# A Mamba state scan laid out as one state by 128 channels, with its inputs in SBUF in float32

## The reference, cut to what matters

```python
xz = x @ W_in
x_e, z = jnp.split(xz, 2, axis=-1)
xc = silu(causal depthwise conv of x_e + conv_b)
x_dbl = xc @ W_x                                    # 64 columns for delta, 16 of B, 16 of C
delta = softplus(x_dbl[..., :64] @ W_dt + b_dt)
Bmat, Cmat = x_dbl[..., 64:80], x_dbl[..., 80:]
deltaA = jnp.exp(delta[..., None] * A[None, None])  # A = -exp(A_log), 256 x 16
deltaB_x = delta[..., None] * Bmat[:, :, None, :] * xc[..., None]
H[l] = deltaA[l] * H[l - 1] + deltaB_x[l]           # for each of 256 channels x 16 states
y = jnp.einsum('bldn,bln->bld', H, Cmat) + xc * D
y = (y * silu(z)) @ W_out
```

## Time and profile before

| | us |
|---|---|
| median of 3 runs | 1796.74 |
| lowest and highest of them | 1787.92, 1796.97 |
| span of the profiled execution, first to last instruction | 1895.4 |
| first and last start of the scan's items on POOL, in that execution | 1079.1, 1564.5 |

### The profile page before, as it was taken

One profiled execution on the slowest core, in us unless ns is written; L12 is line 12 of the kernel. 1 busy time (PEld: TensorE's weight loads), 2 busy tenths in 40 slices (PEclk: granted clock), 3 DMA queues, 4 the chain that ended last, 5 costly groups with the idle time before them and its releaser, 6 DMA issues. The chain is left out here.

```text
span 1895.4 us, 27842 instructions
## 1 busy us (share of the span) xinstructions
PE 1386.3 (73%) x8207; PEld 690.9 (36%) x8208; DVE 1268.0 (67%) x2981; ACT 845.2 (45%) x1215; POOL 881.2 (46%) x775
## 2 busy tenths in 40 slices
PE   4359999999999888766885776775865445546882
PEld 1113333333333555445773221321311003335772
DVE  4666999999983576643332498999989995533333
ACT  3404666666667332213442776484573321112441
POOL 3401121121212645753554169788696664652552
...
DMA packets 218312, 210.68 MB, mean 111 GB/s; under 512 B 49247, under 2 KB 188482, under 8 KB 215874
## 3 DMA queue, kind: packets, MB, share of 16 engines
...
## 5 line engine op out<-in xcount | busy, mean ns | idle before, releaser
L804 ACT ACTIVATE attn_prob<-attn_ps_cols 128x1024 f32<-128x1024 f32 (+1 forms) x320 | 292.1, 940 | 219.5 <-PE attn_ps_cols L680 218.5
L2534 POOL TENSOR_TENSOR ssm_hc<-ssm_h,ssm_cb 128x1024 f32<-128x1024 f32 x128 | 300.6, 2356 | 135.2 <-DVE ssm_h L2517 111.1
L2517 DVE TENSOR_TENSOR_SCAN ssm_h<-ssm_decay,ssm_ps_u 128x1024 f32<-128x1024 f32 x128 | 292.7, 2286 | 29.9 <-ACT ssm_decay L2505 13.7
L830 POOL TENSOR_SCALAR_AFFINE_SELECT attn_prob<-attn_prob 128x512 f32<-128x512 f32 x128 | 81.2, 634 | 415.7 <-ACT attn_prob L804 415.7
L712 DVE CUSTOM_DVE_ANT_0 attn_ps_rows<-attn_ps_rows,const_mask_rows 128x384 f32<-128x384 f32 (+3 forms) x512 | 236.0, 520 | 39.7 <-PE attn_ps_rows L647 37.5
L647 PE MATMUL attn_ps_rows<-attn_ks,attn_qs 72*128 72x512 bf16 (+3 forms) x768 | 228.4, 351 | 44.4 <-DMA attn_qs<-parts_dram 31.2
L2505 ACT ACTIVATE ssm_decay<-ssm_wide,ssm_aneg 128x1024 f32<-128x1024 f32 x128 | 146.1, 1146 | 174.4 <-DVE ssm_h L2517 96.3
L2468 PE MATMUL ssm_ps_u<-ssm_stack,ssm_spread 96*128 96x512 bf16 x256 | 95.9, 465 | 155.3 <-DVE ssm_h L2517 148.5
L680 PE MATMUL attn_ps_cols<-attn_qs,attn_ks 75*128 75x512 bf16 (+3 forms) x768 | 194.3, 333 | 4.7 <-DMA attn_qs<-attn_nrows 4.1
L699 PE MATMUL attn_ps_o<-attn_prob,attn_vw 128*32 128x512 f32 (+3 forms) x1536 | 166.6, 506 | 0.3 <-POOL attn_prob L830 0.3
L717 DVE TENSOR_REDUCE attn_nm<-attn_ps_rows 128x1 f32<-128x512 f32 x256 | 157.8, 681 | 7.8 <-PE attn_ps_rows L647 7.7
...
## 6 DMA issues: line engine op xcount, KB each, us to landing
ssm_wide<-delta_dram SPq DMA_DIRECT2D x128, 512.0 KB, 6.7
...
```

The costliest lines, as they stand in the source:

```text
L804: nc.scalar.activation(prob[u % RING][:, heads[0]:heads[-1] + 1, 0:w], ps_cols[s % 2][:].rearrange("p b (x q) -> p (b x) q", x=len(heads) ...
L2517: nc.vector.tensor_tensor_scan(h[t % H_RING][:], decay[t % DECAY_RING][:], ps_u[t % 2][:], 0.0, ALU.mult, ALU.add).then_inc(scan_done, 1)
L2534: nc.gpsimd.tensor_tensor(hc[:, t % HC_RING, :], h[t % H_RING][:], cb[b % 2][:], ALU.mult).then_inc(hc_done, 1)
```

## The change

The scan's tiles become one state by 128 channels: an item is now a state n and a half ch of the channels, in blocks of four, (ch 0, n even), (ch 0, n odd), (ch 1, n even), (ch 1, n odd).

- delta and u of a whole batch stay in SBUF in float32, channel by channel (`delta`, `u`). The decay is made from `delta` as it lies, so the 128 fetches of `wide`, the split of u into bf16 parts, its stores, stacks and spreading products are gone. The separate products for B and C (`bb`, `cb`) are gone too: `x_dbl` is made as a whole with 96 rows (`xdbc`).
- B and C are now one row for all 128 channels. A row of C is fetched from DRAM over 128 partitions for each state (`cw`, 64 fetches of 512 KB). A row of B is spread by PE into PSUM (`ps_b`) for even states and fetched from DRAM into SBUF (`bw`, 32 fetches) for odd ones.
- The input product goes to a tile in SBUF, `prod` = row of B x u. DVE makes three of a block's four, one item ahead of its scan; POOL makes the fourth (ch 1, n odd) from `bw`.
- The scan reads the decay and `prod`, both in SBUF.
- PE adds each item to `ps_y[ch]` with the identity (two 128x512 products an item), and `hc` has four buffers.

```diff
+PER_BLOCK = 2 * CH
+PAIRS = STATES // 2
+PER_BATCH = PAIRS * PER_BLOCK
 ITEMS = B * PER_BATCH
-WIDE_RING, DECAY_RING, H_RING, HC_RING = 4, 3, 3, 6
+C_RING, B_RING, DECAY_RING, H_RING, HC_RING, PROD_RING = 4, 2, 3, 3, 4, 4
 SUM_LAG = 2
...
+XDBC = DT_RANK + 2 * STATES
...
+def of_item(t):
+    b, s = t // PER_BATCH, t % PER_BATCH
+    return b, s % PER_BLOCK // 2, s // PER_BLOCK * 2 + s % 2
+def by_pool(t):
+    return t % PER_BLOCK == PER_BLOCK - 1
...
+        def spread_b(q):
+            b, n = q // PAIRS, q % PAIRS * 2
+            if n == 0:
+                nc.tensor.wait_ge(bank_kept, kept_by("dr", 2 * b + 1))
+            if q:
+                nc.tensor.wait_ge(dve_made, by_dve((q - 1) * PER_BLOCK + 2))
             for at in (0, UNIT):
-                done = nc.tensor.matmul(ps_u[t % 2][:, at:at + UNIT], spread[:, j].rearrange("p n c -> p (n c)"),
...
+                done = nc.tensor.matmul(ps_b[:, at:at + UNIT], onehot[DT_RANK:, n // 2, :], xdbc[b % 2][DT_RANK:, at:at + UNIT],
+                                        start=True, stop=True)
+            done.then_inc(b_spread, 1)
...
+                    nc.tensor.matmul(ps_y[ch][:, at:at + UNIT], wskip[:, ch, :], gated[b % 2][:, ch, at:at + UNIT],
...
+            nc.tensor.wait_ge(hc_done, t + 1)
             for at in (0, UNIT):
...
+                done = nc.tensor.matmul(ps_y[ch][:, at:at + UNIT], c["ident"][:], hc[:, t % HC_RING, at:at + UNIT],
+                                        start=False, stop=n == STATES - 1, skip_group_check=True)
...
+            b, ch, n = of_item(t)
+            if t % PER_BATCH == 0 or t == 2:
+                act.wait_ge(delta_ready, did(2 * b + 1, 0 if t == 0 else CH - 1))
             if t >= DECAY_RING:
                 act.wait_ge(scan_done, t - DECAY_RING + 1)
...
-            nc.scalar.activation(decay[t % DECAY_RING][:], wide[t % WIDE_RING][:], ACT.Exp, scale=aneg[:, at:at + 1]).then_inc(decay_ready, 1)
+            nc.scalar.activation(decay[t % DECAY_RING][:], delta[b % 2][:, ch, :], ACT.Exp, scale=aneg[:, ch, n:n + 1]).then_inc(decay_ready, 1)
+        def make_product(eng, ops, t):
+            b, ch, n = of_item(t)
+            q = t // PER_BLOCK
+            if t % PER_BATCH in (0, 3) or t == 2:
+                eng.wait_ge(u_ready, did(2 * b + 1, 0 if t == 0 else CH - 1))
+            if t >= PROD_RING:
+                eng.wait_ge(scan_done, t - PROD_RING + 1)
+            if n % 2:
+                eng.wait_ge(b_loaded[q % B_RING], (q // B_RING + 1) * 16)
+                row = bw[q % B_RING]
+            else:
+                eng.wait_ge(b_spread, q + 1)
+                row = ps_b
+            eng.sem_inc(passed, 1)
+            ops.tensor_tensor(prod[t % PROD_RING][:], row[:], u[b % 2][:, ch, :], ALU.mult).then_inc(pool_made if by_pool(t) else dve_made, 1)
         def scan_item(dve, t):
...
-            nc.vector.tensor_tensor(ps_u[t % 2][:], ps_u[t % 2][:], bb[b % 2][:], ALU.mult).then_inc(dbx_done, 1)
             dve.wait_ge(decay_ready, t + 1)
             if t >= H_RING:
                 dve.wait_ge(hc_done, t - H_RING + 1)
-            dve.wait_ge(dbx_done, t + 1)
-            nc.vector.tensor_tensor_scan(h[t % H_RING][:], decay[t % DECAY_RING][:], ps_u[t % 2][:], 0.0,
+            if by_pool(t):
+                dve.wait_ge(pool_made, t // PER_BLOCK + 1)
+            else:
+                dve.wait_ge(dve_made, by_dve(t))
+            nc.vector.tensor_tensor_scan(h[t % H_RING][:], decay[t % DECAY_RING][:], prod[t % PROD_RING][:], 0.0,
                                          ALU.mult, ALU.add).then_inc(scan_done, 1)
         def weigh(pool, t):
...
+            b, ch, n = of_item(t)
+            g = b * STATES + n
+            pool.wait_ge(c_loaded[g % C_RING], (g // C_RING + 1) * 16)
             if t >= HC_RING:
-                pool.wait_ge(y_done, (t - HC_RING) // QUADS + 1)
...
+                pool.wait_ge(y_done, t - HC_RING + 1)
             pool.wait_ge(scan_done, t + 1)
             pool.sem_inc(passed, 1)
-            nc.gpsimd.tensor_tensor(hc[:, t % HC_RING, :], h[t % H_RING][:], cb[b % 2][:], ALU.mult).then_inc(hc_done, 1)
+            nc.gpsimd.tensor_tensor(hc[:, t % HC_RING, :], h[t % H_RING][:], cw[g % C_RING][:], ALU.mult).then_inc(hc_done, 1)
...
+        def load_c(sp, g):
+            b, n = divmod(g, STATES)
+            if n == 0:
+                for k in range(2):
+                    sp.wait_ge(bc_stored[k], (b + 1) * 16)
+            if g >= C_RING:
+                sp.wait_ge(hc_done, last_of_state(g - C_RING) + 1)
             sp.sem_inc(passed_sp, 1)
...
+            sp.dma_start(cw[g % C_RING][:], dram["bc"][b, STATES + n:STATES + n + 1, :].broadcast_to([P, T])).then_inc(c_loaded[g % C_RING], 16)
+        def load_b(sp, q):
+            b, n = q // PAIRS, q % PAIRS * 2 + 1
+            if n == 1:
+                for k in range(2):
+                    sp.wait_ge(bc_stored[k], (b + 1) * 16)
+            if q >= B_RING:
+                sp.wait_ge(dve_made, by_dve((q - B_RING) * PER_BLOCK + 1))
+                sp.wait_ge(pool_made, q - B_RING + 1)
             sp.sem_inc(passed_sp, 1)
...
-            sp.dma_start(wide[t % WIDE_RING][:],
...
+            sp.dma_start(bw[q % B_RING][:], dram["bc"][b, n:n + 1, :].broadcast_to([P, T])).then_inc(b_loaded[q % B_RING], 16)
...
+                for t in range(2):
+                    make_product(dve, nc.vector, t)
+                for n in range(2):
+                    prepare_dve(dve, "delta", n, 1)
+                for n in range(2):
+                    make_u(dve, nc.vector, n, 1)
                 for t in range(ITEMS):
+                    if 1 <= t < ITEMS - 1 and not by_pool(t + 1):
+                        make_product(dve, nc.vector, t + 1)
...
                     weigh(pool, t)
+                    if t % PER_BLOCK == 0:
+                        make_product(pool, nc.gpsimd, t + PER_BLOCK - 1)
```

More of the change, by code:

```diff
@@ L2110, in of_phase @@
+POOL_AT = {0: [("sum", 1)], 2: [("rstd", 1)], 14: [("delta", 0)], 16: [("u", 0)], 19: [("delta", 1)], 21: [("u", 1)],
+           25: [("sum", 2)], 27: [("rstd", 2)]}
+SP_AT = {0: [("residual", 0), ("residual", 1)], 2: [("keep", 1)], 4: [("load", 2)], 8: [("store", 0), ("store", 1)], 12: [("bc", 0)],
+         18: [("bc", 1)], 27: [("keep", 2)], 28: [("load", 3)]}
 def of_phase(table, phase, s):
@@ L2145, in kept_by, with by_dve, last_of_state @@
     return sum((p == "out") == (part == "out") for p, _ in TURNS[:at + 1])
+def of_item(t):
[3 more added lines that the diff above has]
+    return t % PER_BLOCK == PER_BLOCK - 1
+def by_dve(t):
+    return sum(not by_pool(i) for i in range(t + 1))
+def last_of_state(g):
+    b, n = divmod(g, STATES)
+    return b * PER_BATCH + n // 2 * PER_BLOCK + 2 + n % 2
 def scan(nc, dram, c, a, kept, dst):
@@ L2190, in scan @@
         abs_ready, relu_ready, exp_ready, ln_ready, delta_ready, u_ready = (m.sem(n) for n in ("abs", "relu", "exp", "ln", "delta", "u"))
-        delta_stored, split_stored, stacked = m.pair("delta_st"), m.pair("split_st"), m.pair("stacked")
-        delta_begun, split_begun, stack_begun = m.pair("delta_be"), m.pair("split_be"), m.pair("stack_be")
-        high_ready, rest_ready, middle_ready, low_ready = (m.sem(n) for n in ("high", "rest", "middle", "low"))
-        wide_loaded = [m.sem(f"wide{s}") for s in range(WIDE_RING)]
-        u_spread, decay_ready, dbx_done, scan_done, hc_done, y_done = (m.sem(n) for n in ("u_spread", "decay", "dbx", "scan", "hc", "y_done"))
+        bc_stored = m.pair("bc_st")
+        c_loaded, b_loaded = [m.sem(f"c_ld{s}") for s in range(C_RING)], [m.sem(f"b_ld{s}") for s in range(B_RING)]
+        b_spread, decay_ready, dve_made, pool_made, scan_done, hc_done, y_done = (
+            m.sem(n) for n in ("b_spread", "decay", "dve_made", "pool_made", "scan", "hc", "y_done"))
         yg_ready, out_ready = m.sem("yg"), m.sem("out")
@@ L2277, in prepare_pe @@
                 for ch in range(CH):
[L2278 to L2283 removed]
+                    done = nc.tensor.matmul(bank[0:XDBC, :], wx[:, ch, :], gated[b % 2][:, ch, cols(n)], start=ch == 0, stop=ch == CH - 1)
             else:
@@ L2564, in keep_x, with store_bc @@
             sp.dma_start(unit_of(kept, n), x[n % 2][:]).then_inc(x_kept[n % 2], 16)
-        def store_delta(sp, n, ch=CH - 1):
-            at = some(n, ch)
-            sp.wait_ge(delta_ready, did(n, ch))
+        def store_bc(sp, n):
+            sp.wait_ge(bank_kept, kept_by("dr", n))
             sp.sem_inc(passed_sp, 1)
-            said = delta_begun if n < 2 and ch == 0 else delta_stored
-            sp.dma_start(dram["delta"][n // 2, :, cols(n)].rearrange("(c p) t -> p c t", p=P)[:, at], delta_of(n)[:, at]).then_inc(said[n % 2], 16)
@@ L2835, in _ @@
                 nc.gpsimd.memset(power[:], -0.5).then_inc(filled, 1)
-                nc.gpsimd.memset(spread[:], 0.0).then_inc(filled, 1)
-                pool.wait_ge(filled, 3)
-                for r in range(PARTS):
```

(4 more changed lines are left out.)

342 lines of the change are left out of this document (93 added, 249 removed).

## The result

The changed kernel takes 2006.57 us in the median of 4 runs (2001.87 to 2013.96), the kernel before 1795.30 beside it (1787.92 to 1796.97). The ratio is 1.119, with a 95% interval of 1.116 to 1.123: 211 us slower. Forecast were 2014 us and a difference of 217.

The account below looks back on a forecast made before the run. DVE was taken to set the old pace at 3.54 us an item. Mutual exclusion of DVE and POOL reads gives 32 x 21.2 + 38.4 = 717 us against 490.2; with the earlier start 1796.74 + 217 = 2014 us, range 1985 to 2080.

Parts of the forecast that it names:

- Exclusion, the central step: In the items' loop, a scan with two SBUF inputs and a POOL instruction reading SBUF never run together; chance 0.81.
- a subtraction: In the projection, DVE's subtraction reading two SBUF tiles took 3.03 us instead of 1.23 beside POOL's subtraction.
- The block: Four items as a chain of 4 scans, 1 DVE product, 5 POOL instructions: 21.2 us, bounds 20.7 to 23.0.
- POOL's other readers: POOL's six deltas, six u and 4 + 4 sums, now in the same chain: 38.4 us added to the blocks.
- The prologue: From delta's first instruction to the first scan: 7.0 us, so the first scan starts at 1067.0, 9.6 us earlier.
- the row of B: First row of B, needed by 1063.5 in the prologue: taken as hidden, or costing 0.5 us if at 1064.0.
- The sum: First scan to last `weigh`: 32 x 21.2 + 38.4 = 717 us against 490.2; with the earlier start, +217 us.
- PE's busy share: Sign to look for in the profile: PE's busy share should fall; no size given.
- sharing: Rival: the scan leaves SBUF reads free half the time; block 16.4 us, loop 563 us, time 1860 us; chance 0.05.
- PE as the bound: Rival: PE at its lower clock of 1.2 GHz throughout takes 217 us a batch; time 2119 us; chance 0.03.
- The exempt scan: Rival: only the product from `bw` excludes POOL, the scan does not; loop 463 us, time 1760 us; chance 0.11.
- the chance of "faster": Chance that the changed kernel beats the old one: 0.10, from nearly all cases where the scan does not exclude POOL.

## Why the prediction was right, point by point

- **Exclusion, the central step**: right, and shown from three sides (the scan's operand in both directions, and POOL's reads). It was carried over from a subtraction, and holds for a scan: each waits for the whole of the other and then runs 2.14 to 2.15 us (scan, forecast 2.15).
- **The block**: 21.2 us forecast, 20.93 measured in the last batch; 4 x 2.15 + 1.09 + 5 x 2.20 and one hand-over of 0.28 make 20.97. From first scan to first scan the batches take 183.5, 184.3 and 179.5 us and the last one 169.0 to the end of its `weigh`, so the three with preparation are 40.3 us longer in all; 38.4 were put down for POOL's other readers. Against eight blocks, 167.4 us, they are 45 us longer, and the last batch 1.6.
- **The prologue**: 7.0 us forecast from delta's first instruction to the first scan, 1007.52 to 1014.88 = 7.36 measured; the row of B was there in time.
- **The sum**: loop 716 us against 717, difference 211 against 217 us. That the loop came within 1 us is partly luck: 32 blocks were put 9 us too high (0.27 us each), and what lies beside them 8 us too low (47 against 38.4). Loop and prologue together differ by +226 - 9.3 = 217 us in the two traces; 6 us of that are not in the timed medians, and no run shows where they went. The first scan stands at 1014.9 and not near 1067 because the stages ahead of the Mamba block were some 50 us shorter than in the profiled execution of before, which had a span 98.7 us above the timed median (the first instruction of the block stands at 959.2 and 1011.3). Carrying over the difference, and not the place in the span, was right.
- **PE's busy share**, which "should fall", rose: over the loop from 315.39 of 489 us (64%, window 1077 to 1566 of before) to 501 of 713 (70%, the four windows of after together). The loop is longer by 46%, and PE's busy time grew by 59%, with four passes an item instead of its former work and a granted clock of 0.79 to 0.83 (0.78 before). The prediction's own figures already said so, 132 of 182 us against 85.6 of 120. That sign did not bear on the sum.
- **The rivals**: sharing is out (waits are for whole instructions). PE as the bound is out (it stands 207 us for POOL's `hc`, and half the sums change nothing). *The exempt scan* was priced too low, at 1760 us: with the scan's input in PSUM the kernel takes 1847. The price added up DVE's and POOL's instructions and left out PE's place in the chain, although a later paragraph had PE at 132 us a batch, above the 115 (8 x 12.8 + 12.8) that this rival counted for one with preparation. Even with the spread moved ahead it is 1807. Both runs carry the waits of the shared `ps_y`, so whether a scan exempt in the changed kernel itself would have come below 1795 is not shown; no run gives the chance of "faster" a case.
